# Last layer of a gated two-layer block: five lower bounds on GpSimd, and one rescaling on VectorE out of PSUM

## The reference

```
x = x + tanh(g_ffn[1]) * ffn(layernorm(x), weight, bias)

ffn: w_fp8, w_scale = quant_fp8(weight)      # amax over the whole tensor
     x_fp8, x_scale = quant_fp8(x)           # amax over all 8 batches
     acc = x_fp8 @ w_fp8.T
     out = (acc * (x_scale * w_scale) + bias) in bfloat16
```

## Time and profile before

| What | Value |
|---|---|
| median of 3 runs | 363.67 us |
| the profiled execution's own time | 363.35 us |
| its span, first to last instruction | 361.5 us |
| TensorE busy | 335.6 us, 93% |
| VectorE busy | 254.5 us, 70% |
| ScalarE busy | 231.8 us, 64% |
| GpSimd busy | 156.6 us, 43% |
| granted TensorE clock, mean | 1.000 of full speed |

### The profile page before, as it was taken

How to read it: one execution, slowest core, us unless ns; L and a number is a source line. 1 busy time by engine, 2 the same in 40 slices (tenths; PEclk the granted TensorE clock), 3 DMA queues, 4 the chain that set the end, 5 groups by cost and what they waited for, 6 DMA issues and landing times.

```text
span 361.5 us, 8975 instructions
## 1 busy us (share of the span) xinstructions
PE 335.6 (93%) x2905; PEld 266.0 (74%) x2906; DVE 254.5 (70%) x682; ACT 231.8 (64%) x471; POOL 156.6 (43%) x207
## 2 busy tenths in 40 slices
PE   4989988889999999999999998879999999999995
PEld 2668856668999999999999963656666666666774
DVE  1579997965755656545455486977988988787796
ACT  1399977056666666666766433487577777765596
POOL 7098997175655556555565263212033033002000
PEclk9999999999999999999999999999999999999999
DMA  6899983022222222223333116111022000000005
GB/s 183 263 406 424 422 321 117 9 65 55 80 75 73 73 80 80 73 74 73 80 80 73 45 58 178 56 60 60 4 61 60 2 2 2 3 2 3 2 29 203
DMA packets 15338, 36.21 MB, mean 100 GB/s; under 512 B 3526, under 2 KB 6748, under 8 KB 13772
## 3 DMA queue, kind: packets, MB, share of 16 engines
q1 hardware_dynamic: 10508, 24.66, 18.7%
q0 software_dynamic: 3936, 10.48, 10.4%
q10 hardware_dynamic: 864, 0.66, 0.6%
HBM read 22.28 MB, written 13.52 MB: 99 GB/s over the span
## 4 chain that ended last, share of the span: by engine, by line
PE 73%; DVE 8%; DMA 7%; ACT 5%; POOL 3%; issue 2%; SPq 0%; ACTq 0%; DVEq 0%
PE two L1977 15%; PE two L1992 14%; PE two L2131 6%; PE two L2011 4%; PE two L2161 4%; PE two L2196 4%; PE two L2117 4%; PE two L2097 3%; DMA wl<-in_wmoe 2%; PE two L2002 2%; PE two L1826 2%; PE two L1846 2%; PE two L2188 2%; DMA bq_sb<-in_bq 2%; DMA xg<-xn_d,slot_i 2%
## 5 line engine op out<-in xcount | busy, mean ns | idle before, releaser
L1392 DVE SCALAR_TENSOR_TENSOR gate<-th,two 128x512 f32<-128x512 f32 x39 | 26.8, 688 | 56.7 <-ACT th L865 31.0
L613 POOL DMA_INDIRECT y_d<-y_sb,goal_i x39 | 38.5, 987 | 50.2 <-ACT y_sb L875 50.2
L607 POOL DMA_INDIRECT xg<-xn_d,slot_i x39 | 38.0, 975 | 21.3 <-DVE slot_i L1330 9.1
L1977 PE MATMUL two<-wh,gh 128*128 x156 | 44.1, 283 | 0.1
L1977 PE MATMUL two<-wh,gl 128*128 x156 | 43.8, 281 | 0.0
L1977 PE MATMUL two<-wl,gh 128*128 x156 | 43.7, 280 | 0.0
L632 POOL TENSOR_TENSOR rstd<-var,half 128x2 f32<-128x2 f32 x14 | 9.9, 706 | 76.9 <-DVE var L1464 76.9
L854 ACT ACTIVATE xq<-xg 128x256 f32<-128x256 f32 x39 | 23.5, 603 | 30.5 <-DMA xg<-xn_d,slot_i 29.8
L865 ACT ACTIVATE th<-two 128x512 f32<-128x512 f32 x39 | 23.3, 597 | 27.2 <-PE two L1992 27.1
L1497 DVE TENSOR_REDUCE nm<-two 128x8 f32<-128x960 f32 x32 | 36.1, 1152 | 4.5 <-PE two L2117 4.1
L969 ACT ACTIVATE pT<-two 120x1024 f32<-120x1024 f32 x32 | 31.1, 1038 | 7.0 <-PE two L2131 7.0
(11 more groups left out here) (307 smaller groups left out, 856.0 us busy)
## 6 DMA issues: line engine op xcount, KB each, us to landing
wl<-in_wmoe SPq DMA_DIRECT2D x8, 1024.0 KB, 13.3
y_d<-wh SPq DMA_DIRECT2D x4, 1024.0 KB
yg<-y_d SPq DMA_DIRECT2D x7, 512.0 KB, 3.5
xn_d<-x_sb SPq DMA_DIRECT2D x8, 258.0 KB, 7.4
x_sb<-in_x SPq DMA_DIRECT2D x8, 256.0 KB, 6.7
out_x<-of SPq DMA_DIRECT2D x8, 256.0 KB, 2.0
xg<-xn_d,slot_i POOLq DMA_INDIRECT x39, 2.9
y_d<-y_sb,goal_i POOLq DMA_INDIRECT x39, 2.4
```

The source lines that it names most:

```text
L607: pool.indirect_dma_start(xg[:, n % 2, :], None, xn_d, bass.IndirectOffsetOnAxis(ap=slot_i[:, n:n + 1], axis=0)).then_inc(gathered[n % 2], 16)
L613: pool.indirect_dma_start(y_d, bass.IndirectOffsetOnAxis(ap=goal_i[:, n:n + 1], axis=0), y_sb[:, n % 2, :], None).then_inc(y_stored[n % 2] ...
L1392: dve.scalar_tensor_tensor(gate[:, k, :], th[:], 1.0, bank[2 + k][:], ALU.add, ALU.mult).then_inc(gate_ok, 1)
L1977: ins = pe.matmul(bank[6 + k][:, 0:D], (gl if part == 2 else gh)[:, k, a], (wl if part == 1 else wh)[:, bass.ds(e + (C * FF + c * D), D)], ...
```

## The change

GpSimd gets `floored(b)` for batches 3 to 7, at the end of its program; VectorE keeps those of batches 0 to 2. Each one on GpSimd waits for the batch's magnitudes and for the floor before it, so that the count of `yf_ok` still rises in the order of batches. `rescale(6)` is taken from ScalarE; in its place VectorE multiplies the PSUM bank by the same scale into `zf` buffer 2, which is new, and waits for its own result. `rescale(7)` writes buffer 0 and waits for five `add_ffn`. On VectorE, the new instruction stands between `add_ffn(4)` and `add_ffn(5)`.

```
-        zf = sb("zf", [P, 2, 2 * D], BF16)
+        zf = sb("zf", [P, 3, 2 * D], BF16)

+        def z_of(b):
+            return {B - 2: 2, B - 1: 0}.get(b, b % 2)

 # GpSimd, at its end
+            def floored(b):
+                pool.wait_ge(ym_ok, b + 1)
+                pool.wait_ge(yf_ok, b)
+                pool.tensor_scalar(ym[:, b % 4, :], ym[:, b % 4, :], LEAST, None, ALU.max).then_inc(yf_ok, 1)
+            for b in range(3, B):
+                floored(b)

 # ScalarE
             def rescale(b):
                 act.wait_ge(acc_done, b + 1)
-                wait(act, of_ok, b - 1)
-                nc.scalar.activation(zf[:, b % 2, :], bank[4 + b % 4][:], ACT.Copy, scale=red[:, 13:14]).then_inc(zf_ok, 1)
+                wait(act, of_ok, b - 1 if b < B - 1 else B - 3)
+                nc.scalar.activation(zf[:, z_of(b), :], bank[4 + b % 4][:], ACT.Copy, scale=red[:, 13:14]).then_inc(zf_ok, 1)
...
             copy_y8T(7)
-            rescale(6)
             rescale(7)

 # VectorE
             def add_ffn(b):
-                dve.wait_ge(zf_ok, b + 1)
+                dve.wait_ge(zf_ok, b + 1 if b < B - 2 else b)
...
             floored(2)
             push(2)
-            floored(3)
             push(3)
-            floored(4)
             push(4)
             add_ffn(0)
-            floored(5)
             push(5)
             add_ffn(1)
-            floored(6)
-            floored(7)
             push(6)
             add_ffn(2)
             push(7)
             add_ffn(3)
-            for b in range(4, B):
-                add_ffn(b)
+            add_ffn(4)
+            dve.wait_ge(acc_done, B - 1)
+            dve.wait_ge(scale2_ok, 1)
+            then(dve.tensor_scalar(zf[:, z_of(B - 2), :], bank[4 + (B - 2) % 4][:], red[:, 13:14], None, ALU.mult))
+            add_ffn(5)
+            add_ffn(6)
+            add_ffn(7)
```

More of the change, by code:

```diff
@@ L1677, in add_ffn @@
             def add_ffn(b):
-                dve.wait_ge(zf_ok, b + 1)
+                dve.wait_ge(zf_ok, b + 1 if b < B - 2 else b)
                 wait(dve, stored[b % 4], 16 * (b // 4))
-                dve.scalar_tensor_tensor(pair_of(of[:, b % 4, :]), pair_of(zf[:, b % 2, :]), gain[:, 3:4], x_batch(b),
+                dve.scalar_tensor_tensor(pair_of(of[:, b % 4, :]), pair_of(zf[:, z_of(b), :]), gain[:, 3:4], x_batch(b),
                                          ALU.mult, ALU.add).then_inc(of_ok, 1)
```

## The result

The changed kernel takes 366.81 us (median of 8 runs, 365.6 to 369.96), the kernel before 363.5 us (8 runs). The ratio is 1.0083 with a 95% interval of 1.0056 to 1.011: by that ratio 3.0 us slower, 0.8% (the two medians lie 3.3 us apart). The forecast was 364.34 us, no measurable change, with 365.7 as the upper end.

A forecast was written before the change was run, and what follows sets the result against it. Three engines were taken as tied in the tail, the end set by VectorE's last add_ffn. Floors, port and ScalarE's relief counted 0, rescaling on VectorE +0.67: 363.67 + 0.67 = 364.34 us, range 363.3 to 365.7.

The forecast's parts named there:

- GpSimd's floor at 0.61 us, bounds 0.40 and 1.28: Floors of batches 3 to 7 on GpSimd: 0.61 us each, estimated from copy and fill rows; 1.28 from a two-input operation.
- By duration alone the price is 0 at both ends: GpSimd's floors, even at 1.28 us, finish before the pushes that need them, so their length costs 0.
- The port, taken as 0 with 0.3 to 0.45 us a floor: SBUF reads by GpSimd's floors cost VectorE 0.3 to 0.45 us each, offsetting the 0.32 saved; 0 at the end.
- Rival 1: Pushes 3 to 7: SBUF port sharing makes VectorE slower, +1.6 us (365.3) to +5.0 us (368.6); chance 0.20.
- The five floors leaving VectorE gain nothing: Floors of batches 3 to 7 free 1.6 us of VectorE; TensorE waits for no push, so 0, bounds 0 and 0.48.
- The rescaling, +0.67 with the operation at 0.69: rescale(6) on VectorE ahead of add_ffn(5) delays the last add_ffn by 0.67 us, bounds +0.27 and +0.73.
- The three stores: Stores after the last three add_ffn, going out 0.67 us apart: cost 0, bounds 0 and 0.2 us.
- ScalarE's relief, 0: rescale(6) leaving ScalarE gains 0, bounds 0 and 0.02 us, as rescale(7) must wait for linear(7).
- Rivals 2 and 3: First: relief removes TensorE's 0.48 us gap, 363.5 us, chance 0.07; second: VectorE's rescaling takes 0.29 us, 363.9 us, chance 0.08.

The follow-up runs named there:

- run 5: Kernel before plus nine GpSimd operations on tiles of its own behind the last add_ffn, VectorE quiet; floor of 512 bfloat16 elements 1.53 us, copy of 256 0.40 us.
- run 6: Kernel before with only the floors of batches 4 and 6 on GpSimd; ratio 1.0039, last stage 16.79 us against 15.68.
- run 8: Changed kernel with GpSimd copies in place of the five floors, same places and waits; ratio 1.0027 (0.9997 to 1.0058), last stage 16.40 us against 15.68.
- run 4: Kernel before, all floors on VectorE, plus five such GpSimd operations on its own tile that nobody waits for; ratio 1.0057, last stage 17.56 us against 15.68.
- run 2: Kernel before with only the rescaling of batch 6 moved to VectorE, in front of add_ffn(5); ratio 1.0040, last stage 16.38 us against 15.68.
- run 9: Kernel before, same work on the same engines reordered: copy_y8T(2) and pushes earlier, TensorE's biases where it would wait; ratio 0.9969, again 0.9973.
- run 7: Kernel before plus GpSimd fills of its own tile, three for each of five batches, nobody waiting; one execution, last stage 16.28 us against 15.68.

## Why the prediction was wrong

- *GpSimd's floor at 0.61 us, bounds 0.40 and 1.28: this step failed.* It takes 1.53 us alone and 1.97 where a push of VectorE has started before it. I priced an operation with a constant by a copy, which the copy run confirms for a copy (0.61), and I held the two-input row for an upper bound, which run 5 refutes. At 2.13 us a floor the chain of floors is longer than the stage's pitch of 1.48.
- *"By duration alone the price is 0 at both ends"* was not worked out for the tightest batch. I looked at batches 6 and 7; batch 4 has 0.86 us from its magnitudes to its push (run 6). At my own upper bound of 1.28 us the floor would have been 0.4 to 0.5 us too late for it (an estimate: 347.94 + 1.28 = 349.22). With the copies that push waits 0.51 us, starts 0.21 us later in the stage than before (6.44 us in, against 6.23), and nothing of it reaches the end; with a floor of 1.87 us it is 1.14 late, and it does. What 1.28 us would have cost no run shows. (The room of 0.9 us that I gave between `add_ffn(4)` and the end of `linear(6)` is 356.80 - 356.03 = 0.77; nothing hangs on it.)
- *The port, taken as 0 with 0.3 to 0.45 us a floor.* The size for one operation was right (0.34 us), and with short operations it is hidden (run 8). With operations of 1.5 us more of VectorE's fall beside each, and it costs 1.88 us where VectorE keeps its floors (run 4). How the 2.44 us of the floors divide between the floors' own length and the port is not settled. In the change each of VectorE's four longer operations (0.34 us each) stands in front of a wait for a floor, which covers it (the five waits come to 2.8 us); the port's share can enter only by the floors that take 1.97 us and not 1.52, and by the steps of other engines that wait for those operations.
- *Rival 1 was the right sign and place,* with a point of decision at 0.42 us of VectorE's time for each floor and +1.6 to +5.0 us; measured, +3.15. Its mechanism named the port alone and not the late magnitude. I gave it 0.20 in all; the trace had no row of the operation, and I did not let that widen the range.
- *The five floors leaving VectorE gain nothing:* right; run 8 has them gone from VectorE at hardly any cost, and `linear(6)` ends when it did.
- *The rescaling, +0.67 with the operation at 0.69:* right, +0.70 alone, +0.72 in run 8 and 0.71 in the change, with the operation at 0.75, my upper bound. The three stores cost nothing.
- *ScalarE's relief, 0:* right. `rescale(7)` in run 2 waits 0.83 us for `linear(7)`.
- *Rivals 2 and 3* did not occur. The 0.48 us of rival 2 was real, but only an order of the work reached it (run 9), not the relief.
- The rule of the page "SBUF — State Buffer" (the Trainium skill, section "SBUF: two separate sides"), that one of the two is blocked for the whole instruction of the other: the trace agrees that both lose, but `push(2)`, which starts 0.09 us behind a floor of 1.52 us, loses 0.34 us, not 1.4.

## What to carry to other kernels

Before work goes to another engine, its price there must stand in a row of the same operation; a copy, or an operation that seems to need more inputs, is no bound. Where the receiving engine has to do one item per batch, compare its time with the pitch of a batch, and for every batch with the room between the moment its input is ready and the moment its result is needed (0.86 us for batch 4 here); its share of busy time says neither (GpSimd was idle here, and too slow). And on an engine that is full in order, an instruction that waits belongs behind whatever could run in that wait: the same rescaling cost 0.70 us in front of `add_ffn(5)` and 0.07 behind it.

## What the runs showed of the hardware

- GpSimd with a constant operand takes 1.53 us for 128x512 elements in bfloat16 and 1.48 in float32 (run 5); a copy of the same size in bfloat16 takes 0.61 (run 8).
- GpSimd operations that read SBUF lengthen VectorE operations with two SBUF tensors by 0.34 us (0.75 to 1.09; up to 1.16 in run 4), floors and copies alike; fills, which only write, leave those alone and lengthen VectorE's bfloat16 operation with a constant from 0.29 to 0.44 and 0.57 us (run 7).
- In the change the one that starts later pays: a floor on GpSimd that starts 0.12 us behind a push takes 1.97 us instead of 1.52 and leaves the push at 0.75.
